# Attention and mixture-of-experts on one core: the rows' places move from GpSimd to VectorE, the last scatters lie further apart

## What is computed

```python
x = x + xattn(layernorm(x), ctx, ctx, Wq, bq, Wk, bk, Wv, bv, Wo, bo, mask)   # 16 heads, 77 keys
n = layernorm(x)
top_v, top_i = top_k(l2norm(n @ Wp.T) @ l2norm(sim).T / temperature, 2)       # 8 experts, 2 taken
comb = sum(one_hot(top_i, 8) * softmax(top_v)[..., None])
h  = gelu(einsum('bsd,edf->ebsf', n, W1) + b1)                                # 128 -> 512
eo = einsum('ebsf,efd->ebsd', h, W2) + b2                                     # 512 -> 128
x = x + einsum('ebsd,bse->bsd', eo, comb)
```

## Time and profile before

| | before |
|---|---|
| device time, median of 3 runs | 378.99 us (378.09 to 379.06) |
| the profiled execution | 377.77 us |
| its span, first to last instruction | 376.0 us |
| busy: PE, DVE, ACT, POOL | 342.3, 306.0, 290.3, 271.9 us |
| chain that ended last, by engine | PE 54%, DVE 22%, issue 10%, POOL 4%, ACT 3%, DMA 3% |
| `results<-eo,didx` on POOL (L590) | 71 of 996 ns |
| `lists<-rows,slots` on POOL (L457) | 64 of 1042 ns |

### The profile page before, as it was taken

How to read it: one execution, slowest core, us unless ns; L and a number is a source line. 1 busy time by engine, 2 the same in 40 slices (tenths; PEclk the granted TensorE clock), 3 DMA queues, 4 the chain that set the end, 5 groups by cost and what they waited for, 6 DMA issues and landing times.

```text
span 376.0 us, 14240 instructions
## 1 busy us (share of the span) xinstructions
PE 342.3 (91%) x3584; PEld 288.8 (77%) x3585; DVE 306.0 (81%) x972; ACT 290.3 (77%) x847; POOL 271.9 (72%) x506
## 2 busy tenths in 40 slices
PE   7899999999999999999998899999999999999900
PEld 3467777777777777777776699999889999999900
DVE  6778999999999999999999787786556666668884
ACT  4899999999999999999987857665556666666621
POOL 7532487777777877777755468899888878687773
PEclk9999999999999999999999999999999999999965
DMA  3122123321331211120000212222232222249247
GB/s 93 45 82 80 32 72 102 102 64 61 103 97 63 59 44 44 52 72 22 22 25 30 68 45 74 67 68 72 74 86 80 76 71 70 70 133 285 62 117 218
DMA packets 42567, 29.16 MB, mean 78 GB/s; under 512 B 5443, under 2 KB 39311, under 8 KB 42528
## 3 DMA queue, kind: packets, MB, share of 16 engines
q1 hardware_dynamic: 34992, 18.60, 18.3%
q0 software_dynamic: 4320, 8.53, 6.8%
q10 hardware_dynamic: 3216, 1.57, 1.5%
HBM read 17.53 MB, written 11.62 MB: 78 GB/s over the span
## 4 chain that ended last, share of the span: by engine, by line
PE 54%; DVE 22%; issue 10%; POOL 4%; ACT 3%; DMA 3%; DVEq 2%; POOLq 0%; SPq 0%; ACTq 0%
PE ps_s L774 14%; PE ps_s L785 14%; PE ps_t L665 6%; PE ps_o L676 5%; PE ps_s L649 4%; DVE sums L1373 4%; DVE mx L1356 3%; PE ps_s L639 3%; DVE rows L1441 2%; PE ps_t L767 2%; PE ps_x L696 2%; DVE pr L1366 2%; DMA ys<-results 1%; DVE x L1395 1%; DVE st L1405 1%
## 5 line engine op out<-in xcount | busy, mean ns | idle before, releaser
L590 POOL DMA_INDIRECT results<-eo,didx x71 | 70.7, 996 | 19.8 <-issue 13.2
L457 POOL DMA_INDIRECT lists<-rows,slots x64 | 66.7, 1042 | 17.8 <-issue 16.4
L785 PE MATMUL ps_s<-w2s,hT 128*128 x568 | 75.8, 277 | 0.1
L774 PE MATMUL ps_s<-xtT,w1c 128*128 128x128 f32 x568 | 75.5, 276 | 0.0
L1091 ACT ACTIVATE pT<-ps_t 77x512 f32<-77x512 f32 x128 | 73.8, 594 | 0.9 <-PE ps_t L665 0.9
L665 PE MATMUL ps_t<-identf,pr 128*77 128x128 f32 x512 | 72.7, 275 | 0.4 <-ACT pT L1091 0.3
L785 PEld LDWEIGHTS ps_s<-w2s,hT 128*128 128x128 f32 x568 | 69.1, 192 | 0.8 <-issue 0.4
L1189 ACT ACTIVATE w1c<-w1s 128x512 f32 x71 | 44.7, 630 | 31.9 <-PE ps_s L774 29.4
L774 PEld LDWEIGHTS ps_s<-xtT,w1c 128*128 128x128 f32 x568 | 69.0, 192 | 0.1
L1725 DVE TENSOR_TENSOR h<-ps_s,b1T 128x512 f32<-128x512 f32 x71 | 49.1, 691 | 19.4 <-PE ps_s L774 18.7
L665 PEld LDWEIGHTS ps_t<-identf,pr 128*77 128x77 f32 x512 | 58.6, 147 | 6.8 <-issue 4.6
(11 more groups left out here) (220 smaller groups left out, 621.3 us busy)
## 6 DMA issues: line engine op xcount, KB each, us to landing
xt<-lists SPq DMA_DIRECT2D x71, 66.0 KB, 1.9
ys<-results SPq DMA_DIRECT2D x14, 256.0 KB, 4.0
xin<-in_x_dram SPq DMA_DIRECT2D x16, 128.0 KB
w1s<-in_L_ffn_W_dram SPq DMA_DIRECT2D x8, 256.0 KB
w2s<-in_L_ffn_W_dram SPq DMA_DIRECT2D x8, 256.0 KB
out_dram<-x SPq DMA_DIRECT2D x5, 256.0 KB, 6.0
cin<-in_ctx_dram SPq DMA_DIRECT2D x16, 77.0 KB
results<-eo,didx POOLq DMA_INDIRECT x71, 2.4
```

Of the source, the lines that this page charges most:

```text
L457: nc.gpsimd.indirect_dma_start(lists, bass.IndirectOffsetOnAxis(ap=slots[:, r, s * TOPK + k:s * TOPK + k + 1], axis=0), rows[:, r, s, k, : ...
L590: nc.gpsimd.indirect_dma_start(results, bass.IndirectOffsetOnAxis(ap=didx[:, r:r + 1], axis=0), eo[:, r, :], None, bounds_check=TOPK * NTO ...
L774: last = nc.tensor.matmul(ps_s[:, r, c * P:(c + 1) * P], w1c[:, r, c * P:(c + 1) * P], xtT[:, r, :], start=True, stop=True)
L785: last = nc.tensor.matmul(ps_s[:, 2 + r, 0:D], hT[:, r, c * P:(c + 1) * P], w2s[:, bass.ds(e + c * D, D)], start=(c == 0), stop=(c == FC - 1))
```

## The change

`places` leaves POOL and becomes a step of DVE: `places(j)` stands in DVE's `tile(j)` behind the `xtT` copy and ahead of `beside`, the sums and `h`. It waits for `returned` of tile j-8 only. The destinations and `skip` become float32 whole numbers, so `didx` is a float32 addition written as int32. POOL's scatters of pair 14 stand ahead of tiles 7, 10, 13, 16 and those of pair 15 ahead of tiles 19, 22, 25, 28. POOL's loop starts at tile 29. DVE waits for `skip_ready` in place of POOL.

```diff
-        dests = sb("dests", [P, NB, TOPK], i32)
+        dests = sb("dests", [P, NB, TOPK])
-        skip = sb("skip", [P, TT], i32)
+        skip = sb("skip", [P, TT])
...
-            def places(j, m):
-                r = m % FRING
-                after_dma(pool, xt_loaded, j, r)
-                after_dma(pool, returned, j - FRING, r)
-                nc.gpsimd.tensor_tensor(didx[:, r:r + 1], xt[:, r, D:D + 1].bitcast(i32), skip[:, j:j + 1] if known(j) else
-                                        skip[:, bass.ds(j, 1)], ALU.add).then_inc(FE["didx_ready"], 1)
-
             def give_back(j, m):
                 r = m % FRING
-                if has(j, 1, N_TILES):
-                    places(j + 1, m + 1)
...
-                elif j in (7, 9, 11, 13):
-                    k = (7, 9, 11, 13).index(j)
+                elif j in (7, 10, 13, 16):
+                    k = (j - 7) // 3
                     scatter(NP - 2, NP - 2, k // TOPK, k % TOPK)
...
-                elif j in (15, 17, 19, 21):
-                    k = j // 2 - 7
+                elif j in (19, 22, 25, 28):
+                    k = (j - 19) // 3
                     scatter(NP - 1, NP - 1, k // TOPK, k % TOPK)
                     spread(9 + k)
-                elif j == LOOPED + 2:
-                    pool.wait_ge(skip_ready, 2)
-
-            pool.wait_ge(skip_ready, 1)
-            places(0, 0)
-            steps(pool, give_back, 0, N_TILES - 1, LOOPED + 2, N_TILES - 2, FRING, between)
+
+            steps(pool, give_back, 0, N_TILES - 1, LOOPED + 9, N_TILES - 2, FRING, between)
...
+            def places(j, m):
+                r = m % FRING
+                after_dma(dve, returned, j - FRING, r)
+                nc.vector.tensor_tensor(didx[:, r:r + 1], xt[:, r, D:D + 1], skip[:, j:j + 1] if known(j) else
+                                        skip[:, bass.ds(j, 1)], ALU.add).then_inc(FE["didx_ready"], 1)
+
...
+                if has(j, 0, N_TILES):
+                    places(j, m)
                 if known(j):
                     beside(j)
...
             dve.wait_ge(tab_ready, 3)
+            dve.wait_ge(skip_ready, 1)
...
                     dve.wait_ge(tab_ready, 5)
+                    dve.wait_ge(skip_ready, 2)
```

More of the change, by code:

```diff
@@ L446, in _ @@
                            allow_small_or_imprecise_dtypes=True).then_inc(consts, 1)
-            nc.gpsimd.iota(dests[:, :, :], [[P, NB], [NTOK, TOPK]], base=0, channel_multiplier=1).then_inc(consts, 1)
-            nc.gpsimd.iota(fill[:, D:D + 1].bitcast(i32), [[1, 1]], base=SKIP, channel_multiplier=0).then_inc(filled, 1)
+            nc.gpsimd.iota(dests[:, :, :], [[P, NB], [NTOK, TOPK]], base=0, channel_multiplier=1,
+                           allow_small_or_imprecise_dtypes=True).then_inc(consts, 1)
+            nc.gpsimd.memset(fill[:, D:D + 1], float(SKIP)).then_inc(filled, 1)
             pool.wait_ge(consts, N_CONSTS)
@@ L463, in destinations @@
                 settled(pool)
-                nc.gpsimd.tensor_copy(rows[:, r, :, :, D:D + 1].rearrange("p s k o -> p (s k o)").bitcast(i32), pair(dests, J)
+                nc.gpsimd.tensor_copy(rows[:, r, :, :, D:D + 1].rearrange("p s k o -> p (s k o)"), pair(dests, J)
                                       ).then_inc(E["dest_ready"], 1)
```

## The result

| | before | after |
|---|---|---|
| device time, median (4 runs each, one chip) | 378.9 us (378.09 to 379.06) | 374.53 us (373.86 to 375.19) |
| ratio, 95% interval | | 0.9889 (0.9863 to 0.9915) |
| the profiled execution | 377.77 us | 375.19 us |
| its span | 376.0 us | 373.4 us |
| chain that ended last: PE, DVE, issue, POOL | 54, 22, 10, 4% | 58, 21, 9, 2% |

A forecast was written before the change was run, and what follows sets the result against it. PE was taken to wait for tiles in steps 21 to 30, whose loads waited for late POOL's `didx`. -4.07 + 0.60 - 0.13 = -3.60 us, from the median 378.99 to 375.4 us; range 373.8 to 377.5.

The forecast's parts named there:

- The stall, -4.07: PE's steps 21 to 30: loads no longer wait for POOL's didx, so the 4.07 us lost there go.
- POOL's pitch: POOL's returns: 1.48 us each, 1.59 more per scatter; 9.0 us behind PE at tile 28, 3.6 more than it must be.
- The new wait and tile 40, 0: DVE's wait for the return of tile j-8 and SP's load of tile 40 after the last scatter: both cost 0.
- Places on DVE, +0.60: DVE's steps 0 to 3, 0.13 us per place, 0.52 in all, and step 10, 0.08; ends 0.1 and 1.3.
- The last eleven steps, 0: DVE's last eleven steps: the place's 0.13 us barely fits in 0.23 us idle, costing PE 0.
- The end, -0.13: Last returns: 1.48 us each instead of 1.61 and 1.48, so the last starts 0.13 us earlier, at most 0.8.
- The start, 0: Span from its start to PE's step 0: forecast change 0.
- The sum against two times: Whole kernel: -3.60 us in all, giving 374.2 us for the profiled execution and 375.4 us against the median.
- the stall stays: Rival: loads at 258 to 278 us are not freed, or tile 40's load waits; 378.5 to 379.5 us, chance 0.06.
- DVE becomes the bound in part: Rival: places takes 0.30 us with its wait, delaying early steps and the last eleven; 377.3 us, chance 0.12.
- DVE held by POOL's DMAs: Rival: places on DVE must wait for POOL's DMAs, +3.2 us; 382.2 us, chance 0.06.

The follow-up runs named there:

- The spacing alone: Kernel before with only the scatters moved ahead of tiles 7, 10, ... 28 and POOL's loop from tile 29, places still on POOL: 376.9 us, ratio 0.9949.
- the places alone: Changed kernel with the scatters ahead of tiles 7, 9, ... 21 and POOL's loop from tile 22, as before: 375.17 us, ratio 0.9891.
- the slow POOL: POOL's spacing memset 416 columns wide instead of 240, 0.15 us more per tile: 376.93 us on the changed kernel, 383.28 us on the kernel before.
- the gates as one operation: Changed kernel with one scalar_tensor_tensor for the gates instead of two tensor_scalars: 373.22 us; the same with POOL's memset at 416 columns instead of 240: 374.54 us.
- five places: Changed kernel with four more of the same addition in every places(j), into a tile nobody reads: 380.82 us, ratio 1.0042.
- the scatter behind the gates: Changed kernel with POOL waiting for DVE's gates of pair 14 before the third scatter of pair 13: 374.37 us, ratio 0.9886.

## Why the prediction was right, and where its steps were off

The time was right, 375.4 forecast and 374.53 measured, inside the range, by the mechanism forecast. The steps:

- *The stall, -4.07.* Right in cause and nearly in size. The spacing alone and the places alone show the cause from both sides, the slow POOL on either kernel a third time. 3.73 came; the missing 0.33 is step 21 at 2.23 us. It is not a rest of the stall: before has a long step 21 too (2.21), but there PE's weight load waits 0.34 us for the tile, and after no wait is named and the matmuls themselves start up to 0.1 us later than their usual distance. The same 2.23 or 2.22 is there in both kernels with the gates as one operation and in the one with five places, and not with the places alone, the scatter behind the gates or the slow POOL (1.95, 1.95, 2.02). Its cause is open.
- *POOL's pitch.* 1.48 forecast, 1.45 to 1.46 measured; 1.59 and 1.58 for the scatter; 9.0 us behind at tile 28 forecast, 8.0 measured; by the forecast's own 5.4 that is 2.6 us more than it must be and not 3.6, less than a tile and a half. That the new spacing does no harm was right, but it was also needless: the places alone give 0.9891, both 0.9889.
- *The new wait and tile 40, 0.* Right: DVE waits for no return, and no wait for the rows stands ahead of tile 40.
- *Places on DVE, +0.60.* The sum came out at +0.83, near the forecast, and for another reason. The mis-sized term is the 0.13 per place: the next operation starts 0.06 to 0.07 later, and the four exposed places cost at most 0.2 (43.19 against 43.01 where the gates were not held). My reading of the row for it was wrong: the operation at 218.54 waits in the code for the indices that the operation ahead of the 128x2 one gives, and those end at 218.51; the 128x2 one isn't what it waited for. The other 0.6 is the hold of the gates, which no term had. It comes ahead of the first place (217.34 against 219.51), and it can come without the change: with before's own code up to that point it did in one profiled execution of three, with after's in four of four where POOL wasn't made to wait. So few don't tell whether the change makes it likelier.

```profile
218.34 0.17 DVE L1465 FIND_INDEX8 idx<-top,gv 128x8 uint32<-128x8 f32 x1
```

- *The last eleven steps, 0.* Right: steps 30 to 68 take 72.04 us in both, and the place takes 0.15 between `xtT` and the sums.
- *The end, -0.13.* The last return starts 8.13 us behind step 68 and not 8.32: -0.19, so this term holds. The other 0.26 lie in the output transfers behind it.

```profile
355.25 0.97 POOL L582 DMA_INDIRECT results<-eo,didx  x1 [0.17 <-POOL pace L585]
...
356.70 0.97 POOL L582 DMA_INDIRECT results<-eo,didx  x1 [0.16 <-issue]
```

- *The start, 0.* +0.75 in the profiled pair, all within the first 7 us, where the change touches nothing: PE's matmuls there are longer (the first turning one 0.42 us against 0.30) at a granted clock of 1.00 in both. Before's code with the scatters respaced has the same late start (step 0 at 215.28). And before's code with the slow POOL has it (215.34). So the profiled before was an early one; what makes a start early is open.
- *The sum against two times.* The profiled execution came 1.0 above its forecast (375.19 against 374.2): +0.75 of the start, +0.23 of steps 0 to 21, +0.34 of step 21 and -0.32 of the end. Two of these, the late start and the hold of the gates, are things that the profiled before happened to lack; a working made on it can't have them. Against the medians the forecast is 0.9 too high, and for that no profile gives a reason; the forecast gain of 3.6 us lies in the measured interval of 3.2 to 5.2. That 0.83 lies so near 0.60 is luck: a term at least twice too large beside one that was missing.

Of the rivals, *the stall stays* fell with steps 22 to 30. *DVE becomes the bound in part* did not come, and was nearer than I had reckoned: 0.28 more per step makes it true. *DVE held by POOL's DMAs* was half right. The row against it, a sum of 0.34 us in the middle of a DMA, holds for the places too: all 71 took 147 to 211 ns, and 30 of them start inside a DMA of POOL. But DVE's `tensor_scalar` operations can be held, for up to 0.7 us, and I never asked which of DVE's other operations the shifted phases of POOL and DVE would bring against each other.

## What to carry to other kernels

When a ring (a set of buffers used in turn) is held by a small computation on an engine that is late for other reasons, move that computation rather than the engine's load: 0.2 us of work off POOL brought 3.8 us, respacing its DMAs 2.1. Before adding to an engine, compare its step with the bound engine's in each written-out stretch, not in the loop: one operation of 0.07 us per step cost at most 0.2 us in all and four more of them cost 6.3, where the loop would have taken all five. And work out a change on a profiled execution with an eye on what that execution happened to miss, by the start of its main loop and by its longest small operations.

## What the runs showed of the hardware

A DVE `tensor_scalar` from SBUF to SBUF can be held nearly to the end of a POOL indirect DMA instruction that started before it. Held means that it takes longer than the 0.36 us of a free pair. The pairs of gates, by their rows (us):

| kernel | POOL's DMA | gates | they took |
|---|---|---|---|
| before | 216.58 to 217.68 | from 216.58 | 0.36 |
| spacing only | 217.31 to 218.41 | from 217.25 | 0.40 |
| after | 217.24 to 218.34 | 217.34 to 218.31 | 0.97 |
| before, slow POOL | 217.26 to 218.36 | 217.38 to 218.32 | 0.94 |
| after, slow POOL | 216.93 to 218.03 | 217.07 to 218.00 | 0.93 |
| the same, pair 15 | 236.36 to 237.47 | 236.63 to 237.45 | 0.82 |
| five places | 217.18 to 218.28 | 217.37 to 218.26 | 0.89 |
| places only | 217.35 to 218.45 | 217.71 to 218.43 | 0.72 |

In six of these eight rows the gates start 0.10 to 0.36 us into the DMA and end 0.02 to 0.04 before it does; in the two others they start with it or earlier and are free. At pair 14 a tenth of a microsecond of phase is worth 0.6 us.

But this isn't a rule of the phase. The eight profiles of the kernels with two operations for the gates (before, after, the places alone, the spacing alone, the scatter behind the gates, the two with the slow POOL and the five places) have 128 such pairs:

| the pair starts, into a DMA | pairs | free (0.35 to 0.36 us) | held |
|---|---|---|---|
| 0.00 to 0.09 us | 2 | 2 | 0 |
| 0.10 to 0.26 us | 7 | 0 | 5 to the DMA's end (0.82 to 0.97), 2 to 0.44 before it (0.48, 0.49) |
| 0.32 to 0.43 us | 68 | 66 | 2 to the DMA's end (0.64, 0.72) |
| 0.44 to 0.51 us | 31 | 0 | 31 to the DMA's end (0.56 to 0.63) |

The other 20 start outside a DMA or late in one. Before itself has one of the pairs that are let go sooner, the gates of pair 15, 0.17 us into the DMA of 234.47:

```profile
234.64 0.48 DVE L1451 TENSOR_SCALAR gv<-dots,rn 128x8 f32<-128x8 f32 x2
```

And four pairs of the attention half, 5, 7, 9 and 12, are held in all eight profiles, so before has such holds too.

The Trainium skill (SBUF — State Buffer, "Who interferes with whom") has a mechanism: a DVE operation in a two-port mode, which `tensor_scalar` can enter, and GpSimd exclude one another for the whole instruction, and whoever issues first holds the other. The held pairs agree with the exclusion, with POOL as the first. The 66 free pairs that start inside a DMA do not agree with the words "for the whole instruction", and here the measurement decides: the hold does not cover the whole DMA instruction. Which part of it holds stays open. The rows of pair 15 are a further case: in after they start 0.33 us into a DMA of 0.98 and take 0.77, in the kernel with the slow POOL 0.18 us into it and take 1.45. The same section lets a DVE operation with two SBUF inputs contend with a GpSimd instruction that reads SBUF; the 71 places, 30 of which start inside a DMA, show no such hold (at most 211 ns), and neither do the gates as one operation.
